# Cross attention: the key parts of a batch go to the scratch in four column chunks instead of one piece

## What is computed

```python
def _L0_xattn_ref(x, y, Wq, bq, Wkv, bkv, Wo, bo):
    N_HEAD = 16; D_EMBED = 128; D_HEAD = 8
    q = x @ Wq + bq
    k, v = jnp.split(y @ Wkv + bkv, 2, axis=-1)
    # 16 heads of width 8
    attn = jnp.einsum('bhqd,bhkd->bhqk', q, k) * scale
    attn = jax.nn.softmax(attn, axis=-1)
    out = jnp.einsum('bhqk,bhkd->bhqd', attn, v)
    return out.transpose(...).reshape(B, SQ, D_EMBED) @ Wo + bo

x = x + _L0_xattn_ref(_layernorm(x, axis=-1), ctx_768, ...)
```

## Time and profile before

| what | us |
|---|---|
| median of 3 runs | 1686.04 (1684.53 to 1688.87) |
| the profiled execution, device time | 1688.64 |
| its span (first to last instruction) | 1686.5 |
| PE busy / DVE busy / ACT busy | 1451.8 / 1077.7 / 919.7 |
| cross attention, stretch 300 to 1050: PE / DVE / ACT busy | 660.9 / 553.8 / 529.1 |

### The profile page before, as it was taken

One profiled execution on the slowest core, in us unless ns is written; L12 is line 12 of the kernel. 1 busy time (PEld: TensorE's weight loads), 2 busy tenths in 40 slices (PEclk: granted clock), 3 DMA queues, 4 the chain that ended last, 5 costly groups with the idle time before them and its releaser, 6 DMA issues. The chain is left out here.

```text
span 1686.5 us, 29040 instructions
## 1 busy us (share of the span) xinstructions
PE 1451.8 (86%) x10917; PEld 735.4 (44%) x10941; DVE 1077.7 (64%) x2029; ACT 919.7 (55%) x1996; POOL 563.7 (33%) x695
## 2 busy tenths in 40 slices
PE   1577768798989898989899897899999998899998
PEld 1344435233333333333333332566666666544443
DVE  4755543777778686868687781666566654565554
ACT  0223324376777677767778683455555555343433
POOL 4201012030303021120303000788788887233331
PEclk9977878699999899989999995999999999899999
DMA  4222225313232324242323200000000000000001
GB/s 98 62 66 49 54 61 115 67 72 58 69 66 47 99 50 103 50 103 50 103 50 94 45 2 12 1 1 1 1 1 1 1 1 1 7 21 20 21 20 35
DMA packets 76974, 75.01 MB, mean 44 GB/s; under 512 B 12196, under 2 KB 66340, under 8 KB 75940
## 3 DMA queue, kind: packets, MB, share of 16 engines
q1 hardware_dynamic: 76836, 73.16, 19.1%
HBM read 42.47 MB, written 30.16 MB: 43 GB/s over the span
## 5 line engine op out<-in xcount | busy, mean ns | idle before, releaser
L1302 DVE TENSOR_REDUCE b_chunk_max<-psum 128x2 f32<-128x800 f32 x502 | 483.6, 990 | 135.2 <-PE psum L1503 118.2
L1430 ACT ACTIVATE b_prob<-psum 128x512 f32<-128x512 f32 (+1 forms) x832 | 452.9, 595 | 148.2 <-PE psum L1543 132.8
L1543 PE MATMUL psum<-q_stack,k_stack 50*128 50x256 bf16 (+1 forms) x1664 | 288.1, 284 | 29.3 <-ACT b_prob L1430 20.9
L1503 PE MATMUL psum<-k_stack,q_stack 48*128 48x400 bf16 x1004 | 252.1, 350 | 40.4 <-DMA k_stack<-b_k_scratch 35.3
L1513 PE MATMUL psum<-b_prob,b_v_aug 128*32 128x256 f32 (+1 forms) x3328 | 281.1, 411 | 0.0
L1543 PEld LDWEIGHTS psum<-q_stack,k_stack 50*128 50x128 bf16 (+1 forms) x1664 | 103.7, 97 | 213.8 <-ACT b_prob L1430 171.1
L1703 POOL TENSOR_SCALAR c_prob<-c_prob,c_rec 128x128 f32<-128x128 f32 (+1 forms) x256 | 192.5, 771 | 9.2 <-POOL c_kT L1712 8.6
L2118 DVE TENSOR_TENSOR e_hg<-e_gl,e_gate 128x512 f32<-128x512 f32 x124 | 123.3, 1017 | 88.6 <-PE psum L2166 84.0
L1821 ACT ACTIVATE c_prob<-psum,c_mneg 128x128 f32<-128x128 f32 (+1 forms) x256 | 104.3, 419 | 136.2 <-DVE c_mneg L1763 136.2
L1786 DVE SCALAR_TENSOR_TENSOR c_turned<-psum,c_bias,c_tab 128x256 f32<-128x256 f32 x256 | 106.1, 476 | 112.2 <-PE psum L1919 112.2
L2058 ACT ACTIVATE e_gl<-psum,b1T 128x512 f32<-128x512 f32 x124 | 85.2, 687 | 127.6 <-PE psum L2161 123.8
(11 more groups left out here) (236 smaller groups left out, 1947.8 us busy)
## 6 DMA issues: line engine op xcount, KB each, us to landing
k_stack<-b_k_scratch SPq DMA_DIRECT2D x32, 600.4 KB, 10.3
b_k_scratch<-b_kparts SPq DMA_DIRECT2D x7, 1200.8 KB, 4.4
b_k_scratch<-b_kparts SPq DMA_DIRECT2D x7, 800.5 KB, 6.1
b_ctxT<-in_ctx SPq DMA_DIRECT2D x8, 600.4 KB, 12.0
e_w<-in_L_ffn_re_w SPq DMA_DIRECT2D x62, 64.0 KB, 1.9
a_scratch<-a_parts SPq DMA_DIRECT2D x16, 192.0 KB, 2.2
q_stack<-b_q_scratch SPq DMA_DIRECT2D x32, 96.0 KB, 2.2
b_k_scratch<-b_kparts SPq DMA_DIRECT2D x7, 400.2 KB, 6.8
```

What stands on the lines that cost most here:

```text
L1302: nc.vector.tensor_reduce(out=chunk_max[:, half, q, pair:pair + 3:2, c], in_=max_banks(v)[:, :, 0:w], axis=AX.X, op=ALU.max).then_inc(max_ ...
L1430: nc.scalar.activation(prob[0:k, buf, par * 2 * T:(par + 1) * 2 * T], st_bank(par)[0:k, :], ACT.Exp, scale=HD ** -0.5).then_inc(exp_done, 1)
L1503: last = nc.tensor.matmul(max_banks(T_.now("unit"))[:, k, 0:hi - lo], qst[rows, h, q * P:q * P + P], kst[rows, h // 2, lo:hi], start=True, ...
L1543: last = nc.tensor.matmul(st_bank(par)[0:k, (hh // 2) * T:(hh // 2) * T + T], kst[rows, h // 2, n * P:n * P + k], qst[rows, h, :], start=T ...
```

## The change

The copy of a batch's key parts to the scratch, three copies over all 1601 columns behind the fourth chunk's split, becomes twelve copies: three for each chunk, each three behind a wait for that chunk's split. All twelve count on `k_bounced`, so the engines that wait for it (SP, POOL and ACT) wait for 4 x 48 a batch instead of 48. For batch 0, which was bounced by chunks already, only the semaphore changes.

```diff
@@ attend, self attention (batch 0 of the cross attention)
                         sp.wait_ge(early.k_split, c + 1)
-                        bounce_parts(sp, early.k_scr[:, :, lo:hi], early.kparts[:, :, lo:hi], 1,
-                                     early.k_bounced if c == 3 else early.chunks_bounced)
+                        bounce_parts(sp, early.k_scr[:, :, lo:hi], early.kparts[:, :, lo:hi], 1, early.k_bounced)
...
-                    sp.wait_ge(early.chunks_bounced, 3 * BOUNCES * 16)
-                    sp.wait_ge(early.k_bounced, BOUNCES * 16)
+                    sp.wait_ge(early.k_bounced, 4 * BOUNCES * 16)
@@ cross attention
-        DMA_B = BOUNCES * 16
+        DMA_B, K_BOUNCED = BOUNCES * 16, 4 * BOUNCES * 16
@@ SP
             def bounce():
                 wait(sp, stacked, T_.now("stacked"))
                 sp.sem_inc(passed, 1)
-                sp.wait_ge(k_split, T_.up("kchunk", 4))
-                bounce_parts(sp, k_scr, kparts[:], 1, k_bounced)
+                for lo, hi in CHUNKS:
+                    sp.wait_ge(k_split, T_.up("kchunk"))
+                    bounce_parts(sp, k_scr[:, :, lo:hi], kparts[:, :, lo:hi], 1, k_bounced)
                 sp.wait_ge(q_split, T_.up("batch"))
                 bounce_parts(sp, q_scr, qparts[:], 0, q_bounced)
                 sp.wait_ge(q_bounced, T_.up("dma", BOUNCES * 16))
-                sp.wait_ge(k_bounced, T_.now("dma"))
+                sp.wait_ge(k_bounced, T_.up("kdma", K_BOUNCED))
@@ POOL
             def split_k():
-                wait(pool, k_bounced, T_.now("dma"))
+                wait(pool, k_bounced, T_.now("kdma"))
+                T_.up("kdma", K_BOUNCED)
@@ ACT
                     if g == 3:
-                        T_.up("kdma", BOUNCES * 16)
+                        T_.up("kdma", K_BOUNCED)
```

More of the change, by code:

```diff
@@ L383, in __init__ @@
         self.k_scr = nc.dram_tensor("b_k_scratch", [P, NP, SKV], BF16, kind="Internal").ap()
-        self.ones_set, self.half_stacked, self.chunks_bounced = sem("b_ones_set"), sem("b_half_stacked"), sem("b_chunks_bounced")
+        self.ones_set, self.half_stacked = sem("b_ones_set"), sem("b_half_stacked")
         self.var_ready, self.rstd_ready, self.xn_ready = sem("b_var_ready"), sem("b_rstd_ready"), sem("b_xn_ready")
@@ L1187, in prologue @@
             def prologue():
-                for name, by in (("batch", 1), ("kchunk", 4), ("dma", DMA_B), ("stacked", 4 * 16)):
+                for name, by in (("batch", 1), ("kchunk", 4), ("dma", DMA_B), ("kdma", K_BOUNCED), ("stacked", 4 * 16)):
                     T_.up(name, by)
@@ L1255, in prologue @@
             def prologue():
-                for name, by in (("batch", 1), ("kchunk", 4), ("dma", DMA_B)):
+                for name, by in (("batch", 1), ("kchunk", 4), ("dma", DMA_B), ("kdma", K_BOUNCED)):
                     T_.up(name, by)
@@ L1418, in prologue @@
             def prologue():
-                for name, by in (("kchunk", 4), ("kdma", DMA_B), ("batch", 1), ("dma", DMA_B), ("vchunk", 4), ("half", 2)):
+                for name, by in (("kchunk", 4), ("kdma", K_BOUNCED), ("batch", 1), ("dma", DMA_B), ("vchunk", 4), ("half", 2)):
                     T_.up(name, by)
```

## The result

The changed kernel takes 1715.07 us (median of 4, 1713.97 to 1717.91), the kernel before beside it 1687.45 us (4 runs). The ratio is 1.0168, with a 95% interval of 1.0148 to 1.0189: 28 us slower. The forecast was 12.8 us. The measured time lies at the very end of the range (1716), and against the kernel before beside it the loss is 2.2 times the forecast. The sign and the place were right, the size was not. That the time still falls inside the range is luck: its upper end was made of late landings, slow issues and one more stretch at the low clock, and the loss came from none of these.

What follows compares the result with a forecast made beforehand. PE's in-order wait for the key stack's load in the cross attention was taken as the bound. 1.53 + 0.3 = 1.83 us a batch, seven batches, 12.8 us, gave 1699 us, 0.8% slower; range 1691 to 1716.

Steps and rivals of the forecast that it cites:

- The sign and the place: Slower by 0.8%, through PE's seven waits for the key stack in the cross attention.
- late landings, slow issues and one more stretch at the low clock: Additions at the likeliest case's upper end: 5, 6 and 3 us on 1699, giving 1713.
- Step (1): Key copies to the scratch: 800-byte runs need 9.14 us of DMA time instead of 7.61, 1.53 us more a batch.
- Step (2): Start of the key copies: data begins some 0.3 us later a batch, between 0 and 0.4.
- Step (3): SP's nine more DMA issues a batch: query's copies leave 3.2 us later, covered by key data, priced at nothing.
- The second rival: SP's slow issues replace the data as bound: 52 us, 1738, or 31 us, 1717; chance 10%.
- its milder form: Second rival with SP's issues at 0.93 us: 4.5 us later a batch, 31 us, 1717; likelier within its 10%.
- Steps (4) and (5): Three more semaphore waits, already met; the store behind the load moves along with PE; both add nothing.
- Step (6): TensorE's granted clock behind PE's waits: taken as zero; one bad batch more or fewer is 3 us.
- The first rival: Key chunks leave before the stores, so the load goes out 3.0 us sooner: 21 us less, 1665; chance 3%.
- The other two rivals: Key copies each pay their own landing: 207 us, 1893, chance 1%; nothing measurable: 1686 to 1691, chance 13%.

Runs made afterwards that it cites:

- e4: Changed kernel with the copies of chunks 0 to 2 moved ahead of the stores of the maxima in SP's stream; 1655.65 us, 0.9845 of the kernel before.
- e5: Changed kernel with scratch row pitch 3328 bytes and pieces of 384, 384, 384 and 449 columns, all issued behind the fourth chunk; 1698.25 us, 1.0053 of the kernel before.
- e9: Changed kernel with only the scratch's row pitch in DRAM altered, 3328 bytes instead of 3202; 1.0109 of the kernel before.
- e11: Changed kernel with a scratch row pitch of 3330 bytes, chunks still 400 columns; 1.0190 of the kernel before.
- e6: Pieces of 384, 384, 384 and 449 columns, with rows padded to 3328 bytes in the on-chip source, scratch left at 3202; 1.0150 of the kernel before.
- e7: Changed kernel's twelve key copies replaced by six, one whole row of 3202 bytes for each scratch slot, behind the fourth chunk; 1.0017 of the kernel before.
- e1: Changed kernel's twelve key copies replaced by six, one for each scratch slot, each with four 798-byte runs for a partition; 1727.56 us, 1.0267 of the kernel before.
- e8: Kernel before with its three whole key copies moved ahead of the store of the maxima in SP's stream; 1.0058 of the kernel before.
- e2: Changed kernel's twelve key copies cut by partitions, each over all 1601 columns of 32 partitions, runs of 9606 to 3202 bytes; 1.0230 of the kernel before.

## Why the prediction was wrong

**The place and the sign** were right. The chunk waits win nothing, because SP stands behind the stores: shown by the timeline of after, and from the other side by e4, which moves the copies and turns the sign.

**Step (1), the data, failed.** It priced the key and query data at 9.14 us of DMA time from batch 0, and counted that as a rate that holds in a full queue. What was measured is 12.2 us. The term of the sum, the time that the short runs add, was put at 1.53 us a batch and is 3.6 (24.9 / 7, overlapping records counted once). The rate of batch 0 holds only for the first 0.6 to 0.9 MB of runs that start at odd places in DRAM; behind it a packet of 800 bytes takes 62 ns instead of 38. e5 and e9 against e11 and e6 show the cause: where the runs start at multiples of 32 bytes, 9.1 to 9.4 us are needed. In e9, the changed kernel with nothing but another row pitch, the stretches add up to 12.5 us more than before and PE's waits to 12.0 more, which is about my 12.8; its whole time is 18 us more by the ratio, and 6 of these stay unexplained. The trace before did hold a warning: batch 0's chunks never stood in line.

The Trainium skill has a section on this ("DMA: Bandwidth & Descriptors", "How a descriptor splits into AXI transactions"): a transfer that does not start at a multiple of 256 bytes fetches bytes that it does not use. I had not drawn on it. The runs agree that the start matters, but not in its form. The page speaks of bytes that are fetched, and here the written side counts (e5 against e6). Packets that start at a multiple of 32 (e9, 39 ns) are about as good as those of 256 (e5, 38 ns), though e5 is faster as a whole; and odd starts cost nothing before the fall.

**Step (2), the start,** was right in size: data flows from the fourth slice of 0.33 us on, 0.9 us behind the issue, as I had it. The time that the DMA engines don't cover grew by 0.3 us a batch, the 0.3 of the sum.

**Step (3), the issues,** was right for the wrong reason in part: twelve took 7.03 us and not 6.2, the query's copies left at 469.24, and the engines were busy throughout. e7 shows that six cost nothing that can be told, and the stretches of e9, with twelve, leave no room for them beside steps (1) and (2). The second rival, SP's issues as the bound, did not happen, though its milder form (31 us) gave nearly the measured time; whoever had only the time would have believed it. The slices without a gap, e1, and e9 against e11 (twelve issues in both) rule it out.

**Steps (4) and (5)** held: no new wait appears, and of the stretches' 26.9 us, 26.5 pass into PE's waits.

**Step (6), the clock,** held in its sum and by cancelling: behind the seven longer waits the 15 us windows have 986 matmuls in their sum, exactly as many as before. Its bad clock stretch behind 749.4 did not come back, and the others were a little lower. e8, with 30.6 us more of PE's busy time, shows that zero is no rule.

**The first rival,** 21 us faster if the chunks do leave early, was a good price for a kernel that the change is not: 26 us (e4). **The other two rivals** did not happen: the copies overlapped, and the loss was far from unmeasurable.

## What to carry to other kernels

A copy that is cut into pieces only pays if the pieces can be issued earlier: look at what stands ahead of the copy in the issuing queue before looking at what it waits for. Take a DMA rate from a stretch as long and as full as the one to be priced; a burst of 0.6 MB does not tell the rate of 2.4 MB. And if runs of some 800 bytes must go to DRAM, give the rows a pitch, and the pieces a start, of a multiple of 32 bytes. Here that took a third off the loss (e9, 1.0109 for 1.0168) and two thirds with pieces of 384 columns (e5, 1.0053); the whole copies in the same place were still faster.

## What the runs showed of the hardware that I had not expected

- Writes of about 800 bytes at odd starts in DRAM run at about 325 GB/s for 0.8 to 0.9 MB (0.6 in e1) and then at 192 to 242; with starts at multiples of 32 bytes they keep 315 to 322. Runs of 1600 and 3202 bytes at odd starts do not fall (345 and 362 GB/s late). Why the rate falls, and whether bytes, packets or time bring the fall, is open.
- Copies from 32 partitions moved 185 GB/s early in the stretch, where those from 128 moved 385 (e2, with runs of the same three lengths in all). The cause was not looked for.
- Small stores issued right behind 2.4 MB on the same queue took 0.81 to 1.22 us of SP's time each, not 0.56, and PE waited 3 us for them (e8): a small transfer that PE waits for should not be issued behind a large one.
- From a wait of 3.1 us at a round's start on, the clock stood at 0.50 for some 20 us (e8). Behind waits of 7.8 to 9.6 us in the middle of a round (the changed kernel) it was back at 1.00 after 4 to 7 us. What makes the difference was not tried.
